# Softmax denominators in an attention block: who adds a pair's eight key blocks

## The reference

```python
qg = q.reshape(bs, sl, KV_H, FACTOR, HEAD_DIM)
attn = jnp.einsum('bqhfd,bkhd->bhfqk', qg, k) * scale
att = jax.nn.softmax(attn, axis=-1)
a = jnp.einsum('bhfqk,bkhd->bqhfd', att, v)
```

## Time and profile before

| | us |
|---|---|
| median of 3 runs | 2836.54 (2834.50 to 2839.01) |
| profiled execution | 2836.98 |
| its span | 2835.2 |
| PE busy | 2766.4 (98%) |
| DVE busy | 2185.2 (77%) |
| POOL busy | 1915.2 (68%) |
| ACT busy | 1520.1 (54%) |

### The profile page before, as it was taken

The page is one execution under the profiler, slowest core; times in us unless marked ns, Lnnn a source line. Parts: engine busy times, 40 slices in busy tenths (PEclk is TensorE's granted clock), DMA queues, the critical chain, the costliest instruction groups (busy, mean ns, idle before and its releaser), DMA issues.

```text
span 2835.2 us, 48789 instructions
## 1 busy us (share of the span) xinstructions
PE 2766.4 (98%) x14654; PEld 1698.5 (60%) x14654; DVE 2185.2 (77%) x2785; ACT 1520.1 (54%) x2915; POOL 1915.2 (68%) x710
## 2 busy tenths in 40 slices
PE   7999999999999999999999999999999999999998
PEld 4788888874444444444444444444444447888886
DVE  4433333358999999999999999999999968666675
ACT  3211111116766666666666666666667663445543
POOL 2433333318999999999999999999999986111110
PEclk9999999999999999999999999999999999999998
DMA  7544444434444443433444434433433443332331
GB/s 265 182 144 135 143 138 141 143 108 121 94 91 88 93 90 86 95 88 86 92 89 88 94 89 86 94 90 86 95 88 86 99 131 98 112 112 96 105 111 67
DMA packets 167567, 307.60 MB, mean 108 GB/s; under 512 B 49984, under 2 KB 91392, under 8 KB 159360
## 3 DMA queue, kind: packets, MB, share of 16 engines
q1 hardware_dynamic: 158352, 240.05, 29.1%
q0 software_dynamic: 9072, 66.06, 11.4%
HBM read 159.12 MB, written 79.82 MB: 84 GB/s over the span
## 4 chain that ended last, share of the span: by engine, by line
PE 69%; DVE 4%; issue 3%; ACT 1%; POOL 0%; DVEq 0%; ACTq 0%; POOLq 0%
PE back_ps L1304 20%; PE back_ps L1318 16%; PE s_ps L1278 15%; PE s_ps L1789 12%; PE back_ps L1838 2%; DVE mx L1195 2%; PE back_ps L1335 2%; PE back_ps L1810 1%; PE back_ps L1857 1%; ACT p_t L1178 1%; DVE wo_lo L1233 1%; DVE two_sum L1210 0%; PE back_ps L1293 0%; ACT h_t L1646 0%; PE s_ps L1367 0%
## 5 line engine op out<-in xcount | busy, mean ns | idle before, releaser
L1178 ACT ACTIVATE p_t<-back_ps 128x512 f32<-128x512 f32 x2048 | 1114.5, 596 | 479.2 <-PE back_ps L1304 411.9
L1195 DVE TENSOR_REDUCE mx<-s_ps 128x1 f32<-128x1024 f32 x1002 | 1173.1, 1209 | 110.2 <-PE s_ps L1278 101.0
L1102 POOL TENSOR_TENSOR p_sum<-p_sum,p_t 128x2048 f32<-128x2048 f32 x254 | 1165.5, 4588 | 46.2 <-ACT p_t L1178 29.9
L1304 PE MATMUL back_ps<-q_st,k_st 98*128 98x512 f32 x2048 | 814.7, 437 | 18.3 <-ACT p_t L1178 15.8
L1304 PEld LDWEIGHTS back_ps<-q_st,k_st 98*128 98x128 f32 x2048 | 345.4, 188 | 600.3 <-ACT p_t L1178 499.2
L1278 PE MATMUL s_ps<-k_st,q_st 96*128 96x512 f32 x2004 | 637.4, 397 | 6.8 <-DVE mx L1195 6.6
L1318 PE MATMUL back_ps<-p_t,v_sb 128*32 128x512 f32 x4096 | 548.1, 607 | 0.0
L1278 PEld LDWEIGHTS s_ps<-k_st,q_st 96*128 96x128 f32 x2004 | 379.0, 189 | 91.7 <-DVE mx L1195 23.2
L574 POOL TENSOR_TENSOR o_lo<-side,o_hi 128x512 fp32r<-128x512 f32 x80 | 104.1, 1302 | 321.0 <-ACT o_hi L544 320.8
L1102 POOL TENSOR_TENSOR p_sum<-p_t 128x2048 f32<-128x2048 f32 x64 | 313.1, 4893 | 10.4 <-ACT p_t L1178 10.4
L1210 DVE TENSOR_REDUCE two_sum<-p_t 128x512 f32<-128x1024 f32 x256 | 317.0, 1240 | 1.0 <-ACT p_t L1178 1.0
(11 more groups left out here) (151 smaller groups left out, 2904.6 us busy)
## 6 DMA issues: line engine op xcount, KB each, us to landing
p_sum<-two_sum POOLq DMA_DIRECT2D x63, 1024.0 KB, 6.9
q_st<-q_hi_d SPq DMA_DIRECT2D x128, 256.0 KB, 4.3
stage<-w_mod SPq DMA_DIRECT2D x48, 512.0 KB, 6.1
q_hi_d<-o_hi SPq DMA_DIRECT2D x64, 256.0 KB, 2.0
q_lo_d<-o_lo SPq DMA_DIRECT2D x64, 256.0 KB, 2.0
q_st<-q_lo_d SPq DMA_DIRECT2D x64, 256.0 KB, 4.1
att_d<-a_sb SPq DMA_DIRECT2D x128, 128.0 KB, 2.3
a_f<-att_d SPq DMA_DIRECT2D x32, 512.0 KB, 4.6
```

Of the source, the lines that this page charges most:

```text
L1102: nc.gpsimd.tensor_tensor(total, before, p_t[:, kt, :, :], ALU.add).then_inc(sum_done, 1)
L1178: nc.scalar.activation(p_t[:, s, c, :], st_ps[:, c % 2, :], ACT.Exp, scale=SCALE)\
L1195: nc.vector.tensor_reduce(mx[:, slot % 2, e:e + 1], s_ps[:, e % 2, :], AX_X, ALU.max)\
L1304: nc.tensor.matmul(st_ps[:, c % 2, :], k_st[:, slot // 2, s * P:(s + 1) * P], q_st[:, slot, jj, h * QW:(h + 1) * QW], start=True, stop=True)\
```

## The change

Of a pair's eight blocks:
- blocks 0 and 1: a full add on Pool, as before;
- blocks 2 and 3 (`TWO` = 2): half of the columns (c 2 and 3) in two half adds on Pool, the other half (c 0 and 1) in two reductions on DVE in steps 4 and 5, into a `two_sum` of half the size;
- blocks 4 and 5: two full adds on Pool, then a half add of `two_sum`;
- blocks 6 and 7: an accumulating DMA (`merge`) adds block 6 to block 7 in place in `p_t`, and a second one (`join`) adds block 7 to `p_sum`. The merge is issued at the head of the next pair, ahead of its first add, the join behind that add and after the merge has landed.

Blocks 6 and 7 of the last pair are left to TensorE as before (`add_late`).

```diff
-    ADDED = (0, 1, 2, 5, 6, 7)
-    SUMS = len(ADDED) - 1
+    SUMS = 6
+    USED_AT = {0: 1, 1: 1, 2: 2, 3: 3, 4: 4, 5: 5}
     LATE = (6, 7)
-    TWO = 3
-    TWO_STEPS = (5, 6, 7)
+    TWO = 2
+    HALF = REP // 2
+    TWO_STEPS = (4, 5)
...
-                sp.wait_ge(two_done, NPAIR * REP)
+                sp.wait_ge(sum_done, pair * SUMS + 4)
                 sp.wait_ge(num_done, pair * STEPS + 5)
...
+        def merge(pair):
+            pool.wait_ge(num_done, pair * STEPS + STEPS)
+            pool.sem_inc(waited_pool, 1)
+            nc.gpsimd.dma_start(p_t[:, LATE[1], :, :].rearrange("p c q -> p (c q)"),
+                                p_t[:, LATE[0], :, :].rearrange("p c q -> p (c q)"), accum_op=ALU.add)\
+              .then_inc(merged, 16)
+
         def join(pair, par):
+            pool.wait_ge(merged, pair * 16 + 16)
             pool.wait_ge(sum_done, pair * SUMS + SUMS)
-            pool.wait_ge(two_done, pair * REP + REP)
             pool.sem_inc(waited_pool, 1)
             nc.gpsimd.dma_start(p_sum[:, par, :, :].rearrange("p c q -> p (c q)"),
-                                two_sum[:, :, :].rearrange("p c q -> p (c q)"), accum_op=ALU.add)\
+                                p_t[:, LATE[1], :, :].rearrange("p c q -> p (c q)"), accum_op=ALU.add)\
               .then_inc(joined, 16)
 
         def do(pair, slot, it, group):
+            total = p_sum[:, slot % 2, :, :]
+            if not below(pair, 1):
+                merge(pair - 1)
+            pool.wait_ge(exp_done, pair * TILES + 2 * REP)
+            if not below(pair, 2):
+                pool.wait_ge(sum_used, pair - 1)
+            nc.gpsimd.tensor_tensor(total, p_t[:, 0, :, :], p_t[:, 1, :, :], ALU.add).then_inc(sum_done, 1)
             if not below(pair, 1):
                 join(pair - 1, (slot - 1) % 2)
...
+            for n, kt in ((1, TWO), (2, TWO + 1)):
+                pool.wait_ge(exp_done, pair * TILES + (kt + 1) * REP)
+                pool.wait_ge(sum_done, pair * SUMS + n)
+                nc.gpsimd.tensor_tensor(total[:, HALF:REP, :], total[:, HALF:REP, :], p_t[:, kt, HALF:REP, :], ALU.add)\
+                  .then_inc(sum_done, 1)
+            if not below(pair, 2):
+                divide(pair - 2, slot % 2)
+            for n, kt in ((3, 4), (4, 5)):
+                pool.wait_ge(exp_done, pair * TILES + (kt + 1) * REP)
+                pool.wait_ge(sum_done, pair * SUMS + n)
+                nc.gpsimd.tensor_tensor(total, total, p_t[:, kt, :, :], ALU.add).then_inc(sum_done, 1)
+            pool.wait_ge(two_done, pair * HALF + HALF)
+            pool.wait_ge(sum_done, pair * SUMS + 5)
+            nc.gpsimd.tensor_tensor(total[:, 0:HALF, :], total[:, 0:HALF, :], two_sum[:, :, :], ALU.add)\
+              .then_inc(sum_done, 1)
...
+                    if s == LATE[0]:
+                        act.wait_ge(merged, (pair - 1) * 16 + 16)
+                    if s == LATE[1]:
+                        act.wait_ge(joined, (pair - 1) * 16 + 16)
```

More of the change, by code:

```diff
@@ L122, in adaln_block @@
         k_st = keep("k_st", [3 * HD + 2, 2, S], F32R)
-        two_sum = keep("two_sum", [P, 4, 512], F32)
+        two_sum = keep("two_sum", [P, 2, 512], F32)
+        keep("two_room", [P, 2, 512], F32)
         m_at = k_at + 2 * S * 4 + 4 * 512 * 4
@@ L875, in attend @@
     assert PIECES == NPAIR // QR and D == NQW * QW
-    assert KT == NKT and NS == 16 and sorted(ADDED + (TWO, TWO + 1)) == list(range(NKT))
+    assert KT == NKT and NS == 16 and LATE == (NKT - 2, NKT - 1)
     START_PLAN = [(1, e) for e in range(AHEAD - NS, NS)] + [(2, e) for e in range(NS // 2)]
@@ L932, in attend @@
     two_done = sem("two_done")
+    merged = sem("merged")
     joined = sem("joined")
     waited_pool = sem("waited_pool")
-    two_used = sem("two_used")
+    late_used = sem("late_used")
     num_taken = sem("num_taken")
@@ L1050, in do @@
                 sp.wait_ge(sum_done, pair * SUMS + 2)
+                sp.wait_ge(two_done, NPAIR * HALF)
                 sp.wait_ge(num_done, pair * STEPS + 3)
@@ L1161, in do @@
                     act.wait_ge(num_done, (pair - 1) * STEPS + (s + 1))
[L1162 to L1165, removed]
+                    if s in USED_AT:
+                        act.wait_ge(sum_done, (pair - 1) * SUMS + USED_AT[s])
+                    if s in (TWO, TWO + 1):
+                        act.wait_ge(two_done, (pair - 1) * HALF + HALF)
+                    if s == LATE[0]:
+                        act.wait_ge(merged, (pair - 1) * 16 + 16)
+                    if s == LATE[1]:
+                        act.wait_ge(joined, (pair - 1) * 16 + 16)
                 if slot == SPLIT_SLOT and s == HIGH_STEP:
@@ L1208, in add_two @@
             if c == 0 and not below(pair, 1):
-                dve.wait_ge(joined, pair * 16)
+                dve.wait_ge(sum_done, pair * SUMS)
             nc.vector.tensor_reduce(two_sum[:, c, :], p_t[:, TWO:TWO + 2, c, :].rearrange("p s q -> p q s"),
@@ L1217, in divide @@
                 if is_int(pair, NPAIR - 1):
-                    dve.wait_ge(two_used, 1)
+                    dve.wait_ge(late_used, 1)
                 nc.vector.transpose(den_t[:, :, :].rearrange("p c r -> p (c r)"), den_ps[:, :])\
@@ L1244, in do @@
                     max_lo(pair + 1)
-                if s == 0 and not below(pair, 1):
-                    add_two(pair - 1, REP - 1)
                 if s in TWO_STEPS:
@@ L1260, in vector @@
         pairs(dve, do)
-        add_two(NPAIR - 1, REP - 1)
         for pair in (NPAIR - 2, NPAIR - 1):
@@ L1325, in add_sum @@
             if last:
-                pe.wait_ge(sum_done, pair * SUMS + SUMS - len(LATE))
+                pe.wait_ge(sum_done, pair * SUMS + SUMS)
                 pe.wait_ge(den_taken, NPAIR - 1)
@@ L1337, in add_sum, with add_late @@
             done.then_inc(sum_used, 1)
[L1339 to L1344, removed]
+        def add_late():
             for kt in LATE:
@@ L1348, in add_two @@
                                             start=False, stop=kt == LATE[-1])
-            done.then_inc(two_used, 1)
+            done.then_inc(late_used, 1)
         def after(pair, slot, s):
@@ L1411, in tensor @@
         add_sum(NPAIR - 1, (NPAIR - 1) % 2)
-        add_two(NPAIR - 1)
+        add_late()
     return sync, gpsimd, scalar, vector, tensor
```

## The result

The changed kernel takes 2861.9 us in the median of nine runs (2848.7 to 2870.3), the kernel before 2838.1 on the same chip. The ratio is 1.0079, with a 95% interval of 1.0065 to 1.0093: 0.8% slower. Forecast were 2874 us, range 2836 to 2902, slower with a chance of 0.68. The time lies in the range and on the forecast side, but the mechanism forecast does not lie behind it, as the following shows. The nine runs spread over 22 us, where those of the kernel before spread over 6.

A forecast was written before the change was run, and what follows sets the result against it. The prediction took TensorE to set the pace in attention at 26.50 us per pair, DVE and Pool close behind. From 2837.0 us, +0 (DVE), +31.5 (loop) and +6 (end) gave 2874 us, range 2836 to 2902.

The forecast's parts named there:

- the closed loop: Attention pairs: merge, its landing, join and Pool's queued work form a cycle of 27.08 us against TensorE's 26.50; +31.5 us.
- What bounds the kernel: Attention stage: TensorE sets the pace, 26.50 us per pair in the mean, DVE and Pool close behind.
- DVE's part: Steps 4 to 6 of attention pairs: fewer reductions, stalls shift; taken as 0, bounds -12 and +9 us.
- The stall behind the split pair: TensorE's stall of 0.20 us in the pair after DVE's split of output weights, claimed to go.
- Pool's part, the loop: Pool's work per pair falls to 25.8 us, but waiting for the merge's landing makes a loop of 27.08 us.
- the gap of 0.64 ahead of the merge: Idle time on Pool before the merge's DMA issue, counted within the 19.56 us from join to merge.
- The row of 0.66: Profile reading of Pool's idle time ahead of every DMA issue after its last wait, 0.66 us.
- the wait does not bind: Rival in attention: join follows landing by 0.05, or half adds and landing 0.5 us lower; loop at most 26.5, 2841, chance 0.2.
- the free lag: Attention pairs: the division may be 3.2 us late before the put of the maxima holds up TensorE; 3.3 subtracted.
- The end: End of attention: Pool's longer last pair delays the up_w load and DVE's layer norm chain; +6 us, bounds 0 and +8.
- Sum: Whole kernel: profiled 2837.0 us plus 0 for DVE, +31.5 for the loop and +6 for the end gives 2874.

The follow-up runs named there:

- e4: Changed kernel with one more 128x512 Pool operation behind each pair's division, between join and next merge: 2896.5 us, ratio 1.0203.
- e5: Changed kernel with the same additional Pool operation as e4, but right behind the merge's issue: 2869.2 us, ratio 1.0098.
- e1: Changed kernel with DVE's split of the output weights moved to step 0 of slot 2, where Pool waits for exponentials: 2836.6 us, ratio 0.9994.
- e2: Changed kernel with DVE's split of the output weights moved to step 6 of slot 1, within Pool's full add of block 5: 2860.1 us.
- e8: Changed kernel with the split, at its place, made a one-input reduction that copies the weights, low part not computed: 2847.1 us, ratio 1.0020.
- e0: Changed kernel again, unedited, beside the other runs on one chip: 2866.3 us.
- e3: Changed kernel; in the last pair TensorE takes block 5's add and the two_sum half add from Pool, up_w loads one sum earlier: 2863.6 us, ratio 1.0091.
- e6: Changed kernel with the edits of e1 and e3, DVE's reductions in steps 4 and 7, last-but-one division before the up_w wait: 2831.1 us, ratio 0.9962.
- e9: e6 with SP, in the last pair, loading x for the coming stage only after the join has landed: 2831.7 us, ratio 0.9976.

## Why the prediction was right, and where by luck

The time was right by luck. The term that made the forecast, +31.5 us for the closed loop, came to nothing, and a cost that no term and no rival had, the split held up by Pool's adds, took half its place: 15 us in the profiled execution. With the loop's term at 0 the same sum would have given 2843 us. Point by point:

*What bounds the kernel.* Right. TensorE's 26.0 us in a pair without a stall stands after the change as before, with DVE 2.2 us lighter. That removing DVE work is worth only DVE's stalls is borne out.

*DVE's part.* Right in size. Step 6 of a split pair exceeds its median by 0.6 to 0.7 us and the median itself rose by 0.05, 0.7 together; foreseen were 0.90, and 0.03 in the other pairs. The stall behind the split pair (0.20) is gone. Taken was 0, measured is some +2 us.

*Pool's part, the loop.* The mechanism exists and was named with its place (e4 against e5), but a term was too large. Merge to join was estimated at 7.52 and is 7.53 in e4, 7.79 above. Join to merge was estimated at 19.56 and is 18.64. The difference is the gap of 0.64 ahead of the merge, which does not occur, the division with 1.27 from start to start instead of 1.45, and 0.1 of the half adds. The row of 0.66 came from an issue whose last wait was fulfilled last by Pool's own add; I carried it over to an issue whose wait had been fulfilled beforehand. The sum of 27.08 against 26.50 was to give +31.5 us, and 26.1 to 26.4 against 26.5 gives none. The rival "the wait does not bind" was what happened in the loop, but not on the conditions it named: the join follows the landing of the merge by 0.65 us (median), not by 0.05, and landing and half adds came out as estimated. Two sums of the prediction are off by 0.1 us, which changes nothing: Pool's work before adds up to 26.2 us and not 26.1, and the free lag to 3.2 and not 3.3.

*The rival that was missing.* The split was treated as 0.87 us of DVE wherever it stands. It is an operation with two SBUF inputs, and its cost depends on what Pool does at that moment (e1, e2, e8). In the earlier trace rows it starts at 1208.76; Pool's add there began at 1204.57 and took 4.58 us, so it ended at 1209.15, only 0.4 us later, and the split was hardly held:

```profile
1204.57 4.58 POOL L1102 TENSOR_TENSOR p_sum<-p_sum,p_t 128x2048 f32<-128x2048 f32 x1
```

Even there the split of 0.94 us ends 0.55 us behind Pool's add. The change reorders Pool's work and moves DVE's reductions. In 12 of the 16 pairs the split now begins 0.07 to 0.81 us ahead of a full add of 4.6 us, in one 0.94 us behind the start of one, and in the three others it meets a half add. The Trainium skill has this rule: in SBUF — State Buffer, section "SBUF: two separate sides", the ports that DVE and Pool share are an exclusive lock and not a split of bandwidth; a DVE operation with two SBUF inputs and a Pool operation that reads SBUF shut each other out, and whichever starts first holds the ports for its whole instruction. The traces agree on the blocking: 5.29 us against a Pool add that ended at 1330.28, 3.93 us in e2, and never more than 0.69 with one input in e8. On who wins they add something. At 1325 us the split starts 0.15 us ahead of the full add in the changed kernel's trace and in e0's; in both Pool's division, the operation ahead of the add, ends 0.22 us behind the split's start. The split has to wait for the division first, and at its end the add got ahead in one execution and the split in the other. The rule would have told me to ask, of every two-input operation of DVE, which Pool operation it meets before and after the change.

*The end.* +6 foreseen, 8.6 measured. The later load of up_w and the wait of DVE behind it (1.75) are as foreseen. That TensorE's own wait for Pool's last sum costs nothing beside it isn't borne out: it waited 2.82 us, and then worked at a granted clock of 0.50 (16 matmuls of the late sums 2.73 us instead of 1.90). e3 took that wait away and shortened the end by 3.5 us in its trace, though not measurably in the time.

*Sum.* Terms 0 + 31.5 + 6; measured in the profiled pair of executions about +2 (DVE), 0 (loop), +8.6 (end), and 15 for the long splits, of 30.5. The other 5 are the rest of the 4 us in the medians and stalls of 1 to 2 us at the turning of the loop (below). In ratios of the medians: 0.59% collision, some 0.2% end and step 6.

*Left open.* Behind the loop's turning TensorE's clock falls at some places and not at others (0.50 granted from 1284.5 to 1286.5 in the changed kernel): counted by a longer step 1, one in the kernel before, four in the changed one, two in e0, six in e2, four in e3, two in e5 and in e8, three in e6, one in e9, none in e1 and e4. Each costs up to 2 us. Whether the DMAs raise the number can't be told from these counts, and it wasn't tried.

## What to carry to other kernels

Before an order is changed, list the pairs of operations that hold each other up, here DVE's subtraction with two SBUF inputs against Pool's adds (and the normalization against Pool's clearing), and look where each meets its opponent in the new order; place the short one where the long one's engine waits anyway. A gap read ahead of an instruction belongs to what it waited for, not to the instruction: carry it over only where the wait is of the same kind. And when a change makes an engine lighter that wasn't the bound, expect nothing from it but the room that it opens. How much that is here stays open: e6 is 0.4% (11 us) faster than the kernel before, but the kernel before has the same stall of 0.57 us in its split pairs, 15 x 0.57 = 9 us by estimate, and moving the split in that kernel, without the change, wasn't tried.

## What the runs showed of the hardware

- A DVE subtraction of 128x512 with two SBUF inputs takes 0.68 us where Pool is idle, 0.73 when it starts near the end of a Pool operation and 0.14 us before a Pool add (which then takes 5.01 instead of 4.58 us), and up to 5.29 when the add gets ahead. Where it is held, it ends 0.55 us behind the end of Pool's operation, in every trace. The same shape as a one-input reduction took 0.65 to 0.69 at the same place, in all 16 cases, five of them begun within one of Pool's adds.
- One large input is not always safe: a DVE TENSOR_SCALAR of 128x1024 (the normalization, with two columns of scalars beside its input) took 0.81 us beside an idle Pool and 4.05 beside a Pool MEMSET of 3.51, in the kernel before and in e9 alike.
- Whether the subtraction wins turned with the run: at 1325 us the same split of the same kernel took 5.29 in one execution and 0.77 in another, with a start 0.15 us ahead of Pool's in both. The changed kernel's runs spread by 22 us, e1's by 10.
- An accumulating DMA of 1 MB within SBUF, issued by Pool, lands 6.9 us (join) and 7.1 us (merge) after its issue in the median of the changed kernel, 6.8 at least and 9.6 at most; the one of before 6.9 to 7.6. In e6 one took 13.6 us beside 2 MB of loads from HBM; held ahead of these loads in e9, it took 7.9.
- A Pool DMA issue followed its predecessor without a gap where its wait was fulfilled beforehand (the merge), and 0.6 to 0.7 us after the event it waited for otherwise (the join of the kernel before and of the changed one).
- TensorE's granted clock was 0.50 for some 2.5 us behind the stall of 4.33 us in the changed kernel, and from 2361.96 to 2365.30 behind the one of 2.82.
